# Expert stage of a fused time-mix and mixture-of-experts kernel: row loads and the reads of their places on ScalarE's queue instead of SyncE's

## The reference, cut to what matters

```python
x = L0_attn_x                                    # (8, 1024, 256) float32
x = x + _L0_attn_ref(_layernorm(x), ...)         # time mix and channel mix
x = x + _L0_ffn_ref(_layernorm(x), expert_sel, keys, values)

def _L0_ffn_ref(x, expert_sel, keys, values):    # 32 experts, 4 per token
    xt = x.reshape(-1, D)
    gates = sigmoid(einsum('nd,ed->ne', xt, expert_sel))
    sel_val, sel_idx = top_k(gates, 4)
    gate_full = zeros_like(gates).at[arange(N)[:, None], sel_idx].set(sel_val)
    scores = relu(einsum('nd,edf->nef', xt, keys)) * gate_full[:, :, None]
    return einsum('nef,efv->nv', scores, values).reshape(B, S, -1)
```

## Time and profile before

| | |
|---|---|
| median of 3 runs | 1311.43 us (1310.67 to 1311.7) |
| the profiled execution's own time | 1311.79 us |
| its span in the profile | 1309.9 us |
| busy: PE / DVE / ACT / POOL | 91% / 79% / 64% / 61% |
| mean granted clock of PE | 0.965 |
| expert stage | from about 800 to 1200 us |

### The profile page before, as it was taken

How to read it: one execution, slowest core, us unless ns; L and a number is a source line. 1 busy time by engine, 2 the same in 40 slices (tenths; PEclk the granted TensorE clock), 3 DMA queues, 4 the chain that set the end, 5 groups by cost and what they waited for, 6 DMA issues and landing times.

```text
span 1309.9 us, 27758 instructions
## 1 busy us (share of the span) xinstructions
PE 1188.1 (91%) x7372; PEld 1031.5 (79%) x7373; DVE 1034.8 (79%) x2460; ACT 832.6 (64%) x1761; POOL 801.3 (61%) x900
## 2 busy tenths in 40 slices
PE   7799999999999999999999874999999999993765
PEld 6678887888788887878888654999999999992544
DVE  4789889888988898898898677777777777771877
ACT  4468567656856775685676562777777777771443
POOL 2523567666866766686675667677777777774000
PEclk9799999999999999999999985999999999996999
DMA  6001112121221212122121487777666666547999
GB/s 229 1 17 33 57 50 90 65 81 49 81 73 49 89 65 77 53 80 73 49 90 53 146 336 229 226 248 233 204 207 201 209 198 206 175 148 240 411 413 355
DMA packets 119841, 192.80 MB, mean 147 GB/s; under 512 B 17378, under 2 KB 93420, under 8 KB 118384
## 3 DMA queue, kind: packets, MB, share of 16 engines
q1 hardware_dynamic: 82672, 114.03, 27.0%
q0 software_dynamic: 26112, 67.68, 14.2%
q10 hardware_dynamic: 11008, 10.52, 2.3%
HBM read 101.09 MB, written 95.26 MB: 150 GB/s over the span
## 4 chain that ended last, share of the span: by engine, by line
PE 64%; DVE 10%; DMA 9%; ACT 7%; issue 5%; SPq 1%; DVEq 1%; POOL 1%; ACTq 1%; POOLq 0%
PE ps L466 25%; PE ps L1552 11%; DMA ye<-expert_rows 5%; PE ps L1540 3%; PE ps L675 3%; PE ps L669 2%; DMA expert_rows<-y,dest 2%; PE ps L671 2%; PE ps L1533 2%; ACT kr L768 2%; PE ps L613 2%; PE ps L1534 2%; PE ps L1535 2%; PE ps L456 1%; ACT u L798 1%
## 5 line engine op out<-in xcount | busy, mean ns | idle before, releaser
L1663 POOL DMA_INDIRECT expert_rows<-y,dest x288 | 289.1, 1004 | 92.1 <-issue 83.6
L1552 PE MATMUL ps<-xt_hi,keys 128*128 128x128 f32 x1152 | 225.6, 282 | 8.2 <-DVE keys L1621 8.2
L1552 PEld LDWEIGHTS ps<-xt_hi,keys 128*128 128x128 f32 x1152 | 189.7, 195 | 11.9 <-DVE keys L1621 11.6
L1346 POOL DMA_INDIRECT lists<-rows_even,slot x128 | 143.6, 1122 | 42.6 <-issue 38.3
L1346 POOL DMA_INDIRECT lists<-rows_odd,slot x128 | 140.6, 1099 | 42.0 <-issue 39.2
L1552 PE MATMUL ps<-xt_lo,keys 128*128 128x128 f32 x576 | 160.1, 278 | 0.0
L1585 ACT ACTIVATE xt_hi<-ps 128x512 fp32r<-128x512 f32 x144 | 86.3, 599 | 89.2 <-PE ps L1552 86.2
L1632 DVE TENSOR_TENSOR xt_lo<-ps,xt_hi 128x512 fp32r<-128x512 f32 x144 | 99.4, 690 | 40.2 <-ACT xt_hi L1585 39.2
L1621 DVE TENSOR_TENSOR keys<-experts_raw,keys 128x256 fp32r<-128x256 f32 x288 | 109.3, 421 | 16.0 <-issue 14.2
L1582 ACT ACTIVATE keys<-experts_raw 128x256 fp32r x288 | 105.4, 425 | 21.8 <-issue 21.6
L1012 DVE TENSOR_TENSOR k_lo<-ksq,k_hi 128x512 fp32r<-128x512 f32 x128 | 103.2, 822 | 18.7 <-ACT k_hi L777 17.9
(11 more groups left out here) (233 smaller groups left out, 3404.2 us busy)
## 6 DMA issues: line engine op xcount, KB each, us to landing
xr<-lists SPq DMA_DIRECT2D x288, 130.0 KB
ye<-expert_rows SPq DMA_DIRECT2D x32, 1024.0 KB, 21.8
x_sb<-in_x SPq DMA_DIRECT2D x16, 512.0 KB, 3.8
residual<-xp SPq DMA_DIRECT2D x16, 512.0 KB, 4.6
experts_raw<-in_expert_in SPq DMA_DIRECT2D x8, 1024.0 KB, 15.4
resid<-residual SPq DMA_DIRECT2D x4, 2048.0 KB, 12.1
out_dram<-resid ACTq DMA_DIRECT2D x32, 256.0 KB, 11.6
expert_rows<-y,dest POOLq DMA_INDIRECT x288
```

The costliest lines, as they stand in the source:

```text
L1346: pool.indirect_dma_start(lists, bass.IndirectOffsetOnAxis(ap=slot[:, q, n:n + 1], axis=0), rows[q][:, n // TOPK, :], None).then_inc(last_ ...
L1552: mm = pe.matmul(ps[:, H + q % HBANKS, c], keys[:, q, s, half, k * DE:(k + 1) * DE], m[:, q, k, c], start=n == 0, stop=n == 3 * KD - 1)
L1663: pool.indirect_dma_start(expert_rows, bass.IndirectOffsetOnAxis(ap=dest[:, r, s:s + 1], axis=0), y[:, r, s, :], None, bounds_check=OUT_RO ...
```

## The change

SP's loop of row loads is removed. ACT waits where SP did (the ends of the lists, the scatters of the tiles, later the last tile, the fills and the cleared area), issues the loads of steps 0 and 1, and then, at the end of each step i, reads the places of step i + 2 and issues its two loads. The wait for the whole plan moves from ahead of step 8 to ahead of step 6, and the wait for last scatters and fills from SP's step 104 to ACT's step 96. SP issues all 32 fills, four each time `x_ready` has grown by 4. ACT also waits for the stores of x1, since its loads write where these stores read from.

```diff
--- before.py
+++ after.py
@@ -58,6 +58,7 @@
 NSTEPS = UNITS // SUB
 K_LAG, H_LAG, Y_LAG = 1, 2, 4
 LAST_STEP = NSTEPS + Y_LAG
+ROWS_AHEAD = 2
 NBLOCKS = UNITS
 OUT_ROWS = N * TOPK
 W = KD * DE + D
@@ -854,6 +855,8 @@
                                ACT.Copy).then_inc(experts_rounded, 1)
 
         run(act, step)
+        for stored in x1_stored:
+            act.wait_ge(stored, 16 * NT // 2)
 
     over_step = sem("over_step")
     place_summed = sem("place_summed")
@@ -1487,33 +1490,10 @@
             eng.dma_start(lists[bass.ds(row, UNIT), :], zeros[:]).then_inc(filled, 16)
 
     def on_sync(sp):
-        def step(i, r, ring):
-
-            at = of_units(sp, plan_row, i, LIST_ROWS - UNIT)
-            after(sp, x_ready, i - SLOTS + 1)
-            for s, row in enumerate(at):
-                sp.dma_start(xr[:, r % SLOTS, s, :], lists[bass.ds(row, UNIT), :]
-                             ).then_inc(rows_loaded[r % SLOTS], 16)
-
         sp.wait_ge(plan_ready, LIST_ENDS)
-        sp.wait_ge(scattered[0], 16 * NT // 2 * J * TOPK)
-        sp.wait_ge(scattered[1], 16 * (NT // 2 - 1) * J * TOPK)
-        for i in range(FILL_RINGS * RING):
-            if i == RING:
-                sp.wait_ge(plan_ready, PLANNED)
-            step(i, i % RING, i // RING)
-            if i % RING == RING - 1:
-                fill(sp, i // RING * FILLS)
-        with sp.Fori(FILL_RINGS, EARLY // RING) as ring:
-            for r in range(RING):
-                step(RING * ring + r, r, ring)
-
-        sp.wait_ge(last_scattered, 16 * J * TOPK)
-        sp.wait_ge(filled, 16 * E)
-        sp.wait_ge(area_cleared, 16 * (LIST_ROWS - OVERFLOW) // UNIT)
-        with sp.Fori(EARLY // RING, NSTEPS // RING) as ring:
-            for r in range(RING):
-                step(RING * ring + r, r, ring)
+        for n in range(E // FILLS):
+            after(sp, x_ready, RING // 2 * n)
+            fill(sp, n * FILLS)
         sp.wait_ge(pe_step, LAST_STEP)
         for n in range(RESID_AHEAD, RESID_PIECES):
             load_resid(sp, resid, residual, resid_loaded[1], n)
@@ -1567,14 +1547,7 @@
         loop(pe, step, drain=Y_LAG)
 
     def on_scalar(act):
-        ends = []
-
         def step(i, r, ring):
-            fills = isinstance(i, int) and i < FILL_RINGS * RING
-            if fills and r == 0:
-                e = FILL_SP + i // RING * FILLS
-                _, ends[:] = nc.values_load_multi_w_load_instructions(
-                    fill_row[0:1, e:e + FILLS], engines=(act.engine,), min_val=0, max_val=OVERFLOW - UNIT)
             if enters(i):
                 q = r % SLOTS
                 experts = of_units(act, plan_expert, i, E - 1)
@@ -1594,17 +1567,40 @@
                 after(act, sent[q], 16 * SUB * (ring if r >= Y_LAG else ring - 1))
                 act.activation(y[:, q].rearrange("p s d -> p (s d)"), ps[:, Y + q % YBANKS, :],
                                ACT.Copy).then_inc(ycopy_ready, 1)
-            if fills and r % (RING // FILLS) == 1:
-                act.dma_start(lists[bass.ds(ends[r // (RING // FILLS)], UNIT), :], zeros[:]).then_inc(filled, 16)
+
+        def load_rows(i, r, ring):
+
+            after(act, x_ready, i - SLOTS + 1)
+            for s, row in enumerate(of_units(act, plan_row, i, LIST_ROWS - UNIT)):
+                act.dma_start(xr[:, r % SLOTS, s, :], lists[bass.ds(row, UNIT), :]
+                              ).then_inc(rows_loaded[r % SLOTS], 16)
+
+        def ring_of(i, r, ring):
+
+            if i == RING - ROWS_AHEAD if isinstance(i, int) else False:
+                act.wait_ge(plan_ready, PLANNED)
+            step(i, r, ring)
+            if not isinstance(i, int) or i + ROWS_AHEAD < NSTEPS:
+                load_rows(i + ROWS_AHEAD, (r + ROWS_AHEAD) % RING, ring + (r + ROWS_AHEAD) // RING)
 
         act.wait_ge(plan_ready, LIST_ENDS)
-        for i in range(FILL_RINGS * RING):
-            if i == RING:
-                act.wait_ge(plan_ready, PLANNED)
-            step(i, i % RING, i // RING)
-        with act.Fori(FILL_RINGS, NSTEPS // RING) as ring:
+        act.wait_ge(scattered[0], 16 * NT // 2 * J * TOPK)
+        act.wait_ge(scattered[1], 16 * (NT // 2 - 1) * J * TOPK)
+        for i in range(ROWS_AHEAD):
+            load_rows(i, i, 0)
+        for i in range(RING):
+            ring_of(i, i, 0)
+        with act.Fori(1, EARLY // RING - 1) as ring:
             for r in range(RING):
-                step(RING * ring + r, r, ring)
+                ring_of(RING * ring + r, r, ring)
+        act.wait_ge(last_scattered, 16 * J * TOPK)
+        act.wait_ge(filled, 16 * E)
+        act.wait_ge(area_cleared, 16 * (LIST_ROWS - OVERFLOW) // UNIT)
+        with act.Fori(EARLY // RING - 1, NSTEPS // RING - 1) as ring:
+            for r in range(RING):
+                ring_of(RING * ring + r, r, ring)
+        for i in range(NSTEPS - RING, NSTEPS):
+            ring_of(i, i % RING, i // RING)
         for i in range(NSTEPS, NSTEPS + Y_LAG):
             step(i, i % RING, i // RING)
```

## The result

The changed kernel takes 1368.67 us (median of 4 runs, 1363.21 to 1373.21) against 1311.57 us for the kernel before beside it (4 runs, 1310.67 to 1313.65). The ratio is 1.043, with a 95% interval from 1.0403 to 1.0457: **57 us slower**. Its profiled execution took 1369.62 us with a span of 1367.8 us, 57.9 us more than the span before.

The account below looks back on a forecast made before the run. ACT's queue was taken to become the bound, meeting a too-short load lead at 3.0 us a step: 138 steps +59.1 us, POOL's tail -10.1, start 0, so +49 on 1311.79, 1360 us as median; range 1326 to 1388.

Parts of the forecast that it names:

- POOL's tail: After the last y copy: last scatter starts about 2.7 us later instead of 12.8, giving back 10.1 us.
- The bound: Expert steps: ACT's queue, with 1.30 us spare and 1.8 us added a step, becomes the bound at 2.93 us.
- The queue's step: ACT's queue per expert step: 0.5 plus a 0.6 us read plus 1.8 us moved work plus 0.03 branch, 2.93 us.
- The second loop, lead of the loads: ACT's release through load to PE's products: 5.85 us for two steps, 2.93 each; with the queue's loop, 3.0 a step.
- rival 2: Expert steps: heavier coupling up to 892 us, 24 steps at 3.25 and 114 at 3.1 us; 1378 us; chance 0.20.
- rival 3: Expert steps: PE's clock falls, a third of the steps at 1.2 GHz, 41 us more, 1401 us; chance 0.07.
- other sign named for POOL: In the expert steps, POOL would wait for y of ACT instead of "issue", as a sign the forecast is right.
- Start: Before the sixth step: ACT's waits, first loads and keys cost 0 to 0.5 us, covered by DVE's planning; 0 in the sum.
- 1 (only the queue): Expert steps: loads land early enough, only ACT's queue binds at 2.93 us a step, 1351 us; chance 0.23.
- 4 (the queue runs ahead): Expert steps: ACT's queue hands out keys and xt_hi while issuing, so no change, 1311.4 us; chance 0.04.
- 5 (faster): Expert steps: fewer colliding reads and quicker issues and loads give 2.6 us a step, below break-even 2.645; 1305 us; chance 0.04.
- 6: Whole change: it does not do what it says, a cost elsewhere hiding it; no chance of its own.

Follow-up runs that it names:

- ahead3_third: The changed kernel with row loads issued three steps ahead instead of two, ACT's queue doing the same work: 1340.21 us, 1.0222 of before.
- one_unit_each_again: Against the changed kernel: ACT issues one unit's load per step, three steps ahead, SP the other unit's and all fills: 1315.84 us, 1.0032 of before.
- sp_two_ahead_again: The kernel before, with SP's loads held until PE's step that releases ACT in the changed kernel; ACT's queue unchanged: 1369.64 us, 1.0453 of before.
- read_ahead: The changed kernel plus an unused read of plan_row, which was absent from the program that ran, so a repeat: 1367.84 us, 1.0433 of before.
- read_twice: The changed kernel with plan_row read once for each of the two loads, a third read per ACT step: 1434.75 us, 1.0947 of before.
- fills_on_sp: The kernel before with all 32 fills on SP, four after each four steps, none on ACT: 1497.87 us, 1.0004 of before on a 1500 us chip.

## Why the prediction was right, and what was off

The forecast was 1360 us (range 1326 to 1388), slower with 0.92. It came out slower, at 1368.7: inside the range, just above the band of 1356 to 1368 that had the chance of 0.42. The mechanism, a full queue and a lead too short, was right. That the number came so near is in part luck, since POOL's tail and the steps missed in opposite directions. Point by point:

- **The bound.** Right: ACT's queue took the place of PE, as its waits, its timeline and the chain show, and ahead3_third (queue alone, +28) and one_unit_each_again (queue relieved, +4) settle it. The rule weighed in the prediction (the Trainium skill, "DMA: Bandwidth & Descriptors", section "Issuing engines are not separate DMA queues"), that issuing elsewhere saves only sequencer time and that this is usually small, holds in what it says of an issue: 0.34 us here, small beside its load of about 3 us. But two of them with their read cost 28 us, since the queue they went to had only 1.3 us free in a step and the one they left had nothing else to do.
- **The queue's step.** Predicted 2.93 us, measured 2.74 (ahead3_third, steady). The mis-sized term is the reads, taken at 0.6 us each; the medians in the changed kernel are 0.49 and 0.50:
```profile
L1458 ACTq TENSOR_LOAD <-plan_row x144: 478/490/900, 801.3 to 1233.8; - x144
L1458 ACTq TENSOR_LOAD <-plan_expert x144: 486/498/1533, 804.6 to 1236.8; - x144
```
The step of 1003 us has 2.58 us with both at the median. In the steady steps of ahead3_third the reads' means are 0.56 and 0.52, together 0.12 us below the 1.2 of the sum: the single rows around 985 us (0.667 and 0.576) had been given too much weight. Most of the rest is 0.1 us between the read of plan_expert and that of plan_row (1005.49 to 1005.99, 0.50 us where the sum has 0.5 + 0.1); against it stand a few waits of the queue.
- **The second loop, lead of the loads.** Predicted 2.93 us a step, with the two loops meeting at 3.0. Measured alone on SP 2.83 (sp_two_ahead_again, steady), both together 2.90 steady and 2.98 over all 138 steps: 410.6 us from the sixth to the last xt_hi, where 414 was predicted. Both loops were 0.1 to 0.2 shorter than in the prediction. In the loop of the lead it was the way from the release to the first issue: 0.75 us on SP where the sum for ACT had 0.95, while the other two parts, 2.96 and 1.96, came as read (2.97 and 1.93). Together the loops cost 0.07 us more than the longer and 0.16 more than the shorter one. That 410.6 came so near 414 is in part luck: shorter loops and slower early steps cancel.
- **Early steps.** 3.27 us, where the forecast had 3.0 and rival 2 (heavier coupling up to 892 us) 3.25. Rival 2 was right for this stretch and wrong for the rest (3.1 predicted, 2.90 found). Part of it is rival 3, the clock, at a small size: over 800 to 892 us the granted clock is 0.81 where it was 0.88, under the 0.95 that the prediction named as a sign of rival 3, though before was under it there as well. Windows of the two stretches at half clock inside the steps (columns as above):
```profile
845.40:852.20 6.80, 6.05 (x29) 6.05 (x30) 3.04 (x11) 2.14 (x6) 2.40 (x4) 0.50 0.37 118
910.30:913.70 3.40, 3.40 (x18) 3.40 (x18) 1.96 (x6) 1.99 (x5) 2.28 (x3) 0.50 0.48 157
```
10.2 us at 0.50, at most 5 us lost. Ahead of the first, PE had been standing for loads (0.34 us at 841.35 among others). read_ahead, the same instructions, has one such stretch of 3.4 us among its steps and still takes 3.18 us an early step, so most of the excess is not the clock; what it is stays open. ahead3_third, 2% slower and not 4, shows no such stretch between 820 and 1219 us.
- **POOL's tail.** This term failed: -10.1 predicted, -5.1 measured (7.7 us from the last y to the last scatter, where the prediction asked for less than 3). The sum had the last scatter follow the last y by one handover and one scatter. The last scatters and the last y copies:
```profile
1252.41 0.99 POOL L1659 DMA_INDIRECT expert_rows<-y,dest  x1 [0.30 <-issue]
1253.70 0.98 POOL L1659 DMA_INDIRECT expert_rows<-y,dest  x1 [0.30 <-issue]
```
```profile
1244.15 1.08 ACT L1568 ACTIVATE y<-ps 128x512 f32<-128x512 f32 x2
1246.01 0.60 ACT L1568 ACTIVATE y<-ps 128x512 f32<-128x512 f32 x1 [0.78 <-PE ps L1515]
```
In the drain no keys, reads or key products are left, so three y copies come between 1244.15 and 1246.01, and each is 2.58 us of scatters, 1.29 apiece. POOL falls behind in the drain however slow the steps before it were: with 3.29 us a step (read_twice) it is again 7.7 us. The other sign named for POOL, that it would wait for y instead of "issue", did not show either: its idle time for "issue" grew from 0.31 us a time (75.7 in 246) to 0.44 (115.1 in 263), and its waits for ACT's y are 6.6 us in 3.
- **Start.** First to sixth xt_hi +1.9 us, where 0 to 0.5 was predicted; +0.8 in read_ahead. The +3.5 us ahead of the first xt_hi are not the change's: read_ahead, the same instructions, has its first xt_hi at 802.6 us, before has 802.9.
- **End of the span.** +3.3 us between the last scatter and the end was in no term. ahead3_third and sp_two_ahead_again have the same 114 us, one_unit_each_again 111.5. It goes with the shorter distance of the last scatter from PE's last step, behind which SP starts loading resid; that the loads of ye then meet those loads is a guess that was not tried.
- **Rivals.** 1 (only the queue) would have needed a longer lead; ahead3_third is that case, at 1340. 4 (the queue runs ahead) falls: keys stand behind both issues in every step. 5 (faster) needed 2.645 us a step; the queue alone takes 2.74. (The single reads of 0.667 and 0.576 us are 1.4 and 1.2 times the shortest, not "half as much again"; and ACT's reads did come down to about 0.49 in the median, which was not enough.) 6 falls by the 288 issues on ACT's queue, named in the timeline.

The sum again, as it came: +3.5 +1.9 +55.7 -1.4 -5.1 +3.3 = +57.9 us of span. Against the predicted +49 that is 8.9 more: the tail 5.0, the start 5.4 (3.5 of it not the change's) and the end 3.3, less 3.4 us by which the steps stayed below 414 and 1.4 in the drain.

## What to carry to other kernels

Before moving DMA issues or register reads to another engine, add up that engine's queue for one step: reads, issues and the operations it hands out, one after another, whatever the engine's busy share. ACT was 23% idle here and its queue still overflowed, by 0.3 us a step. Then count how far ahead of its use each load leaves: a lead that falls short of issue, flight and use (two steps, 4.95 us, for a loop of 5.7) cost another 28 us here, and one more step of lead, for which a buffer was free, gave them back. Last, do not take a register read at one length: on the same queue its median was 0.49 us in one kernel and 0.76 in another.

## What the runs showed of the hardware

**Chips differ.** Four of the chips ran the kernel before in 1498 to 1524 us, the others in 1311 to 1312, steadily in each case. Each chip was used at one time only, so whether it is the chip or the time isn't told apart. Ahead of the expert stage they differ little: the first xt_hi comes at 813 to 818 us instead of 803 to 806. The expert stage makes the difference. Windows of fills_on_sp (whose ratio to before on its chip was 1.0004):
```profile
500.00:800.00 300.00, 275.47 (x1434) 224.48 (x1432) 238.12 (x508) 183.08 (x330) 195.50 (x224) 0.95 0.30 107
892.00:1180.00 288.00, 251.17 (x1668) 248.43 (x1666) 141.67 (x451) 145.63 (x376) 155.55 (x151) 0.78 0.47 144
```
PE's mean granted clock is 0.78 in the second window (1.00 in the earlier trace rows): for much of it the clock goes 13.7 us at half and 10.2 us at full in turn. Steps come in pairs, one long and one short, in ACT's timeline:
```profile
1120.35 0.61 ACT L1578 ACTIVATE xt_hi<-ps 128x512 fp32r<-128x512 f32 x1
...
1126.43 0.60 ACT L1578 ACTIVATE xt_hi<-ps 128x512 fp32r<-128x512 f32 x1 [4.10 <-PE ps L1552]
...
1128.27 0.61 ACT L1578 ACTIVATE xt_hi<-ps 128x512 fp32r<-128x512 f32 x1
```
PE's records show that the product ACT waited for started at 1122.98, 3.45 us before ACT went on, and that PE ran a whole further step meanwhile; PE's matmul ends are modelled, so how long it really took stays open, as does the cause. Loads of 1 MB of expert weights took 23.4 us from issue to landing there, and 15.2 to 16.6 us in the traces from the other chips. It matters for reading results: the same change is 4.3% slower on one kind of chip and 0.5% faster (interval 0.2 to 0.8%) on the other.

**A register read** of two values takes 0.48 to 0.50 us in the median on ACT and on SP, in the kernel before and in the changed one, and up to 1.5 us. Moving the read of plan_row from SP to ACT left ACT's own read of plan_expert as it was in the median (0.502 before, 0.498 after). It is no constant: in read_twice the median for plan_expert was 0.560, and in one_unit_each_again ACT's two reads had 0.760 and 0.668, while SP's stayed at 0.476.
